# Value products two units at a time in the two grouped attentions of a decoder, output products two units behind

## The reference, cut to what matters

```
x = layernorm(x + attention(x))                    # 32 heads of 16, ALiBi
x = layernorm(x + grouped_cross_attention(x, c))   # "B": 32 query heads, 8 KV heads, rotary
x = layernorm(x + routed_lora_ffn(x))
x = layernorm(x + grouped_attention(x))            # "D": 32 query heads, 8 KV heads, causal
x = layernorm(x + cross_attention(x, c))
x = layernorm(x + quantised_swiglu_ffn(x))

# B, head size 128, four query heads share a KV head
q = rotary(x @ Wq); k = rotary(c @ Wk); v = c @ Wv
p = softmax(where(mask == 0, -1e9, q @ k.T / sqrt(128)))
y = (p @ v) @ Wo
# D: the same without rotary, c = x, causal mask
```

## Time and profile before

| | us |
|---|---|
| median of 3 runs | 1655.85 (1654.79 to 1658.16) |
| the profiled execution | 1656.58 |
| its span in the profile | 1654.7 |
| TensorE busy in it | 1582.0 |
| VectorE busy | 970.2 |
| ScalarE busy | 665.4 |

### The profile page before, as it was taken

How to read it: one execution, slowest core, us unless ns; L and a number is a source line. 1 busy time by engine, 2 the same in 40 slices (tenths; PEclk the granted TensorE clock), 3 DMA queues, 4 the chain that set the end, 5 groups by cost and what they waited for, 6 DMA issues and landing times. The chain is left out here.

```text
span 1654.7 us, 22796 instructions
## 1 busy us (share of the span) xinstructions
PE 1582.0 (96%) x8512; PEld 1270.0 (77%) x8512; DVE 970.2 (59%) x1958; ACT 665.4 (40%) x1218; POOL 178.4 (11%) x134
## 2 busy tenths in 40 slices
PE   7999899999999999998989999999999999889998
PEld 6776777887787778776877788788878877777876
DVE  5998677757765775767424533452553346256655
ACT  4784443434433443434233323332332323346541
POOL 8101400000000000000240000000000000613330
PEclk9999999999999999999999999999999999999999
DMA  5110111101100110100111100110110100202221
GB/s 217 53 40 27 65 36 42 52 1 52 62 16 27 51 44 8 52 26 2 45 53 51 52 26 26 49 52 0 51 63 13 38 14 26 79 10 85 79 83 51
DMA packets 25883, 75.18 MB, mean 45 GB/s; under 512 B 3874, under 2 KB 4610, under 8 KB 25540
## 3 DMA queue, kind: packets, MB, share of 16 engines
q1 hardware_dynamic: 25412, 72.90, 13.1%
q0 software_dynamic: 384, 1.05, 0.2%
HBM read 71.84 MB, written 2.10 MB: 45 GB/s over the span
## 5 line engine op out<-in xcount | busy, mean ns | idle before, releaser
L83 PE MATMUL bankY<-sb_Dwo,sb_DoT 128*128 128x512 f32 x768 | 193.9, 402 | 0.3 <-DVE sb_DoT L1121 0.3
L83 PE MATMUL bankY<-sb_Bwo,sb_BoT 128*128 128x512 f32 x768 | 193.6, 401 | 0.2 <-DVE sb_BoT L1121 0.2
L83 PE MATMUL bankA<-sb_xT,sb_Bwq 128*128 128x512 f32 x768 | 191.6, 399 | 0.0
L83 PE MATMUL bankA<-sb_xT,sb_Dwq 128*128 128x512 f32 x768 | 189.9, 396 | 0.0
L83 PEld LDWEIGHTS bankY<-sb_Dwo,sb_DoT 128*128 128x128 f32 x768 | 141.0, 189 | 42.2 <-issue 13.3
L83 PEld LDWEIGHTS bankY<-sb_Bwo,sb_BoT 128*128 128x128 f32 x768 | 141.0, 189 | 41.9 <-issue 12.9
L83 PEld LDWEIGHTS bankA<-sb_xT,sb_Bwq 128*128 128x128 f32 x768 | 143.4, 190 | 34.3 <-issue 2.7
L83 PEld LDWEIGHTS bankA<-sb_xT,sb_Dwq 128*128 128x128 f32 x768 | 142.2, 188 | 33.9 <-issue 2.7
L1052 DVE TENSOR_TENSOR sb_BqT<-bankA,sb_Btable 128x512 f32<-128x512 f32 x64 | 44.3, 692 | 153.0 <-ACT sb_Bsw L949 153.0
L1088 DVE TENSOR_TENSOR sb_xtok<-sb_xtok,bankY 128x512 f32<-128x512 f32 x128 | 87.1, 681 | 54.6 <-PE bankY L83 54.5
L949 ACT ACTIVATE sb_Bsw<-bankA 64x512 f32<-64x512 f32 x160 | 94.8, 593 | 54.8 <-PE bankA L83 51.6
(11 more groups left out here) (286 smaller groups left out, 2917.8 us busy)
## 6 DMA issues: line engine op xcount, KB each, us to landing
sb_raw<-in_w_attn SPq DMA_DIRECT2D x80, 512.0 KB, 3.4
sb_raw<-in_q_gu SPq DMA_DIRECT2D x22, 256.0 KB, 2.7
sb_raw<-in_q_d SPq DMA_DIRECT2D x11, 256.0 KB, 2.6
sb_raw<-in_wqk SPq DMA_DIRECT2D x8, 256.0 KB, 2.6
sb_rawx<-in_xT SPq DMA_DIRECT2D x4, 512.0 KB, 6.8
sb_raw<-in_ctxT SPq DMA_DIRECT2D x4, 512.0 KB, 6.0
sb_xtok<-in_x_tok SPq DMA_DIRECT2D x1, 2048.0 KB, 12.7
sb_raw<-in_ctx_tok SPq DMA_DIRECT2D x4, 512.0 KB, 3.8
```

Of the source, the lines that this page charges most:

```text
L83: last = nc.tensor.matmul(out, lhs, rhs, start=start and i == 0, stop=stop and i == len(pairs) - 1)
```

## The change

Each `oT` tile (high, low) now holds two units. `attend` issues the value products of units u-1 and u together at odd u, four matmuls in a row, into the two halves of each `bankO` row. Units listed by `alone` stay single: in B units 0, 1, 8 and 9, and in the last turn of both attentions units 10 to 15. The output product of a unit now follows two units later instead of one, ahead of the value product; units 6 and 7 of a half (14 and 15) are both put out at its end. ScalarE's copy and VectorE's subtraction take the 1,024 elements of a pair at once. On ScalarE the exponential of unit u+2 now stands ahead of the copy of V's result, and the square roots for four tiles of the next normalisation (`ln_roots(..., 0)`) move from unit 14 to unit 15 of the last turn. The residual additions come one unit later.

```diff
@@ -741,7 +741,7 @@
             V = sb(mem, f"{tag}V", [P, NT, 2 * HD])
             sc = [sb(mem, f"{tag}sc{i}", [P, 2, 2, S]) for i in range(4)]
             pt = [sb(mem, f"{tag}pt{i}", [P, GROUP * S]) for i in range(2)]
-            oT = [[sb(mem, f"{tag}oT{i}{p}", [P, GROUP, 2, S], F32R) for p in range(2)] for i in range(2)]
+            oT = [sb(mem, f"{tag}oT{p}", [P, 2, GROUP, 2, S], F32R) for p in range(2)]
             mx = sb(mem, f"{tag}mx", [P, 2, 4]); sm = sb(mem, f"{tag}sm", [P, 2, 4]); ri = sb(mem, f"{tag}ri", [P, 2, 4])
             if rope:
                 sw = [sb(mem, f"{tag}sw{i}", [P, HALF]) for i in range(2)]
@@ -758,6 +758,26 @@
             for i, (q, o) in enumerate(zip(halves(wq, "p h k n -> p (h k n)"), halves(wo, "p h n -> p (h n)"))):
                 dst[f"q{i}"] = dst[f"q{i + 2}"] = q
                 dst[f"o{i}"] = dst[f"o{i + 2}"] = o
+
+            def side(v):
+                return slice(v % 2 * GROUP * S, (v % 2 + 1) * GROUP * S)
+
+            def of_pair(i):
+                return oT[i][:].rearrange("p v h b q -> p b (v h) q")
+
+            def of_unit(i, v):
+                return oT[i][:, v % 2].rearrange("p h b q -> p b h q")
+
+            pair_bank = bankO[:].rearrange("p b (h q) -> p b h q", q=S)
+            unit_bank = lambda v: bankO[:, :, side(v)].rearrange("p b (h q) -> p b h q", q=S)
+
+            def alone(u, final):
+
+                return (rope and u % NT < 2) or (final and u >= 10)
+
+            def attended(u, last):
+
+                return (u,) if alone(u, last) else (u - 1, u) if u % 2 else ()
 
             def run(engine, start, turn):
 
@@ -871,12 +891,26 @@
                             pe.wait_ge(w_low, part.block("o3" if u else "o1"))
                         pe.wait_ge(o_low, part.unit(u) + 2)
                         pe.wait_ge(y_done, part.unit(u) + 1)
-                        pairs = [x for h in range(GROUP) for x in three([o[:, h].rearrange("p b q -> p (b q)") for o in oT[u % 2]], [w[:, h, :] for w in wo])]
+                        pairs = [x for h in range(GROUP) for x in three([o[:, u % 2, h].rearrange("p b q -> p (b q)") for o in oT], [w[:, h, :] for w in wo])]
                         if u % NT == NT - 1:
                             product(bankY[u % 2][:], pairs[:len(pairs) // 2], stop=False).then_inc(wo_used, 1)
                             product(bankY[u % 2][:], pairs[len(pairs) // 2:], start=False).then_inc(y_ready, 1)
                         else:
                             product(bankY[u % 2][:], pairs).then_inc(y_ready, 1)
+
+                    def attend(part, u):
+
+                        units = attended(u, part.final)
+                        if units and u < NT:
+                            pe.wait_ge(v_done, part.it * 4 + u // 2 + 1)
+                        for v in units:
+                            if v == units[0]:
+                                pe.wait_ge(pt_done, part.unit(u) + 3)
+                                pe.wait_ge(o_low, part.unit(v) + 1)
+                            for b in range(2):
+                                rows = slice(S * b, S * b + S)
+                                done = nc.tensor.matmul(bankO[:, b, side(v)], V[rows, v % NT, v // NT * HD:(v // NT + 1) * HD], pt[v % 2][rows, :], start=True, stop=True)
+                            done.then_inc(o_ready, 1)
 
                     def start(part):
                         if rope:
@@ -898,22 +932,14 @@
                             done.then_inc(t_ready, 1)
                             if banks and banks[0][0] == "S" and not late(u):
                                 project(part, banks[0])
-                            if late(u):
-                                output(part, u - 1)
-                            if u < NT and u % 2 == 0:
-                                pe.wait_ge(v_done, part.it * 4 + u // 2 + 1)
-                            pe.wait_ge(pt_done, part.unit(u) + 3)
-                            pe.wait_ge(o_low, part.unit(u) + 1)
-                            for b in range(2):
-                                rows = slice(S * b, S * b + S)
-                                done = nc.tensor.matmul(bankO[:, b, 0:GROUP * S], V[rows, u % NT, u // NT * HD:(u // NT + 1) * HD], pt[u % 2][rows, :], start=True, stop=True)
-                            done.then_inc(o_ready, 1)
-                            if u % NT and not late(u):
-                                output(part, u - 1)
+                            if u % NT >= 2:
+                                output(part, u - 2)
+                            attend(part, u)
                             for x in banks:
                                 if x[0] != "S" or late(u):
                                     project(part, x)
                             if u % NT == NT - 1:
+                                output(part, u - 1)
                                 output(part, u)
                     run(pe, start, turn)
                     ln_tensor(pe, norm + 1, EARLY)
@@ -1002,19 +1028,23 @@
                                 exp(part, u + 1)
                             if len(banks) == 1:
                                 queries_or_keys(part, banks[0])
-                            act.wait_ge(o_ready, part.unit(u) + 1)
-                            nc.scalar.activation(oT[u % 2][0][:].rearrange("p h b q -> p b h q"),
-                                                 bankO[:, :, 0:GROUP * S].rearrange("p b (h q) -> p b h q", h=GROUP), ACT.Copy).then_inc(o_high, 1)
                             if not late(u) and (u + 2 < SLOTS or not part.final):
                                 exp(part, u + 2)
+                            units = attended(u, part.final)
+                            if units:
+                                act.wait_ge(o_ready, part.unit(u) + 1)
+                            if len(units) == 1:
+                                nc.scalar.activation(of_unit(0, u), unit_bank(u), ACT.Copy).then_inc(o_high, 1)
+                            elif units:
+                                nc.scalar.activation(of_pair(0), pair_bank, ACT.Copy).then_inc(o_high, 2)
+                            if part.final and u == SLOTS - 1:
+                                ln_roots(act, norm + 1, 0)
                             if u in VALUES_AT and not part.final:
                                 values(part, VALUES_AT[u])
                             if u in SPLIT_AT:
                                 weights_high(part, SPLIT_AT[u])
                             for x in projected_last(u, part.final):
                                 queries_or_keys(part, x)
-                            if part.final and u == SLOTS - 2:
-                                ln_roots(act, norm + 1, 0)
                             if part.final and u == SLOTS - 1:
                                 ln_rest(act, norm + 1)
                     run(act, start, turn)
@@ -1115,11 +1145,15 @@
                             in_turns(rotate(part, *banks) if rope and banks else None,
                                      None if late(u) else scores,
                                      back(part, u + 1) if u + 1 < SLOTS or not part.final else None)
-                            if u % NT >= 2:
-                                residual(part, u - 2)
-                            dve.wait_ge(o_high, part.unit(u) + 1)
-                            nc.vector.tensor_tensor(oT[u % 2][1][:].rearrange("p h b q -> p b h q"), bankO[:, :, 0:GROUP * S].rearrange("p b (h q) -> p b h q", h=GROUP),
-                                                    f32(oT[u % 2][0][:]).rearrange("p h b q -> p b h q"), ALU.subtract).then_inc(o_low, 1)
+                            if u % NT >= 3:
+                                residual(part, u - 3)
+                            units = attended(u, part.final)
+                            if units:
+                                dve.wait_ge(o_high, part.unit(u) + 1)
+                            if len(units) == 1:
+                                nc.vector.tensor_tensor(of_unit(1, u), unit_bank(u), f32(of_unit(0, u)), ALU.subtract).then_inc(o_low, 1)
+                            elif units:
+                                nc.vector.tensor_tensor(of_pair(1), pair_bank, f32(of_pair(0)), ALU.subtract).then_inc(o_low, 2)
                             if u % NT == 0:
                                 weights_low(part, "o3" if u else "o1")
                             if u in SPLIT_AT:
```

More of the change, by code:

```diff
@@ L1129, in turn @@
                             if u % NT == NT - 1:
+                                residual(part, u - 2)
                                 residual(part, u - 1)
```

## The result

Eight runs of the changed kernel give a median of 1667.15 us (1661.68 to 1669.81), eight of the kernel before 1656.87 (1654.79 to 1658.74). The ratio is 1.0059, with a 95% interval of 1.0048 to 1.0070: 10 us slower. The forecast was 1671, in a range of 1657 to 1683.

What follows compares the result with a forecast made beforehand. TensorE, busy 1582.0 of 1654.7 us, was taken as the bound. D -12.6, B +19.9 and the clock +8.0 gave +15.3 on 1656.58, 1671.9; the median lies 0.7 lower, so 1671, range 1657 to 1683.

Steps and rivals of the forecast that it cites:

- D, forecast -12.6: Plain attention, stage D: 29 fewer value groups -11.6, pair waits +2.4, last unit's tail -3.4; sum -12.6 us.
- The price of a group: Both attentions: a value group costs 0.40 us beside its columns, range 0.33 to 0.43.
- That +0.3 a half: Stage D: unit 6's output product waits for the pair's copy and subtraction, +0.3 us x 8 halves, +2.4.
- B (a): B's half starts: S of unit 12 comes 0.4 us earlier, not 2.8, idle 2.6; +2.4 a half, +18.3 in all.
- B (b): B has 21 fewer value groups: 14 values from late units cost +6.0 us, the other seven give -2.8.
- (c): B: unit 6's output product waits behind the pair of units 6 and 7, +0.6 us x 4 turns, +2.4.
- B (d): B's tail: unit 13's output product covers the 2.21 us wait before the last unit's value product; -4.0 in all.
- The clock: B: idles of 2.6 us at seven half starts make the clock fall; five falls x 1.6 us, +8.0.
- A (no fall): Rival: the clock does not fall after B's idles of 2.6 us; 1663 us, chance 0.20.
- B (second unit at 0.64): Rival: weight loads of a pair's second unit are not hidden, so it costs 0.64 us; +10.5, 1681, chance 0.10.
- C (no chain): Rival: at B's half starts ScalarE and VectorE move up with TensorE by 2.8 us; 1645 us, chance 0.12.
- D (1656): Rival: gains and losses cancel, with half of B (a) and no clock loss; 1656 us, chance 0.06.

Runs made afterwards that it cites:

- the lag alone: Changed kernel with every unit's value product single, no pairs, outputs still two units behind: 1665.37 us, ratio 1.0048.
- weight block: Changed kernel, but in B's units 1 and 9 the weight block is split ahead of ScalarE's exponential, its low part ahead of that of `oT`: 1654.29 us.
- exponential: Changed kernel, but in B's units 1 and 9 the exponential of unit u+2 is taken one unit later, behind the half copies: 1654.57 us.
- the probabilities first: Changed kernel, but in B's units 1 and 9 VectorE finishes the next unit's probabilities before its rotary and mask: 1666.04 us, ratio 1.0056.

## Why the prediction was right, point by point

Its mechanism held: S of unit 12 did not follow the output product that was taken away, TensorE idled in front of it, and the clock fell behind some of these idles. That the total came within 4 us is in part luck; the paragraph on the sum has the errors that offset each other.

**D, forecast -12.6, measured -14.3.** The price of a group held: the lag alone gave -5.6 and the pairs -8.7 more. 29 groups x 0.40 is 11.6, and 2.7 of it goes back at the half starts. That +0.3 a half was right in size and wrong in place: it is not unit 6's output product but unit 0's that waits for the pair's two long operations, 0.33 in each of eight halves, and the copy moved forward took 2.7 out of the stage. The tail gave 4.6 in the last half, 3.4 was forecast.

**B (a), forecast +2.4 a half, measured +2.0.** The step held: S did not follow the output product that was taken away. T of unit 9 to S of unit 12 is 11.1, forecast 11.4; back to back, ScalarE's copy takes 0.48 of its queue, not 0.60, and its block 0.95, not 1.04. The experiments on its links (weight block, exponential) each took 0.9 out of it, down to what a late unit takes anyway. One step was right and incomplete: the idle of 1.0 in unit 9 was forecast before T of unit 10, for the probabilities, and T does start 0.05 behind them. But the query projection in front of it waits 0.90 for a bank, which I did not have, so the idle shows there and taking the probabilities' wait away frees nothing. That the two are equally long is luck; two later expectations, which took only the probabilities forward, failed on it.

**B (b), forecast +3.2, and (c), +2.4.** In the last turn's first half, where the clock did not fall, the half is 3.06 longer; the lag alone accounts for 1.97, so pairs cost 1.1 there, 0.4 in a second half (85.23 against 84.83). Four and three such halves are 5.6, as forecast for (b) and (c) together (5.6). The output product of unit 6 stands 3.45 behind its projection instead of 2.89, 0.57 a turn for the 0.6 forecast.

**B (d), forecast -4.0: mis-sized.** The last half is 4.6 shorter though it carries its own (a), so with the +1.3 forecast for that it was -2.7 against -4.6. But 2.6 of it, 0.9 at the last residual addition and 1.7 by the clock, comes back in the next stage, and 0.9 behind D as well. I had priced a wait that goes; the later square roots stand in the change and I gave them no price, nor did I ask where the clock would fall instead.

**The clock, forecast five falls and +8.0, measured four, +6.2.** A half with a fall is 1.54 longer than one without (86.77 and 85.23). Stage B had one before, behind the turn's start, and one in its last outputs; it has five now, and none in its last outputs. With an idle of 1.94 to 2.02 before S (the probabilities first) one in seven did; with the edits that leave 1.2 to 1.55 there, none.

**The rivals.** A (no fall) fails by those four. B (second unit at 0.64) fails: 0.42 by the row of the pair. By the rule of the Trainium skill that I had quoted there ("TensorE: Matmul & The Clock Gate", section "The mechanism") the loads of one row group should have shown; the measurement decides against such a cost here. The rows of before could have told it: weight loads of 1270.0 us and matmuls of 1582.0 in a span of 1654.7, so most loads, and most of them fill all 128 rows, lay beside matmuls already. C (no chain) fails by S at 15.8 after T of unit 8, where it asked for 13.7. D (1656) fails by the measured time and by both of its terms.

**The sum.** +15.3 was 4 too high against the +11.2 of the profiled execution. The stages lost 8.5 less than forecast: D 1.7; in B (a) 3.0 over seven halves, the last half 1.9, the clock 1.8. Against that stand +4.4 outside the stages that the forecast did not have (4.8 - 1.8 + 1.4).

## What to carry to other kernels

Taking a product out of TensorE's stream gains its time only if the next instruction that waits for another engine was not already waiting; look at the two places where the stream shortens, and walk the chain behind them through every engine's queue. Taking one wait away shows nothing where a second one ends at the same time (unit 9). Price every instruction that the diff moves, the square roots at the tail too. The same edit gained 12 us in the stage without a rotary and lost 22 in the one with it, so a change for two callers of one function is priced for each. Where an engine is idle just before its queue becomes critical, one operation moved into that idle (weight block, copy) gave at most its own length there, 0.9 of 1.05, and only down to the next chain; the falls of the clock that went with it were worth as much again.

## What the runs showed of the hardware

The same idle of 2.1 us on TensorE, seven times in one execution, was followed by 1.2 GHz four times and by 2.4 GHz three times; in the change in B alone five times and twice. After 1.94 to 2.02 us it was once in seven, after 1.2 to 1.55 us never, in the half starts of the others. That is no bound: in three kernels a projection in the first half of B waited 1.94, and behind one of these waits the clock fell; the idle of 1.35 in front of B's very first value product was followed by 1.2 GHz in four of the 13 traces, and stalls of 1.57 to 1.88 at a turn's start in eight of 16. A fall in a half of B cost 1.54 us.

The eight runs of the changed kernel spread over 8.1 us, those of the kernel before over 4.0. The mean granted clock of the two fastest runs of the changed kernel (1661.68 and 1662.29) was 0.989 and 0.991, that of the other six 0.984 to 0.987. One stretch of 3.4 us at half clock is 0.001 of the span, so more falls go with a longer run; which ones they were is not known, since one execution of each kernel has a trace.

A second value product, whose weights go into the same halves of the rows as those of the product still in work, cost no more than its columns, 0.42 us for two matmuls of 256 columns in two passes each; all eight loads of the pair passed within 0.73 us beside its matmuls.
